# A two-layer Flamingo kernel: four more key and value units among the BitNet tiles, and three pairs of PSUM banks for the tiles instead of four

## What is computed

```python
x = x + tanh(g_xattn[0]) * L0_xattn(layernorm(x), ids, ctx, ctx, ctx)   # experts whose weights are the context
x = x + tanh(g_ffn[0])   * L0_ffn(layernorm(x), w_gate, w_up, w_down)   # BitNet: ternary weights, Hadamard
x = x + tanh(g_xattn[1]) * L1_xattn(layernorm(x), ctx, Wq, Wk, Wv, Wo)  # 16 heads of 128, 8 batches of 128
x = x + tanh(g_ffn[1])   * L1_ffn(layernorm(x), gate_w, ...)            # 32 routed experts, top 8, and a shared one

# L0_ffn:  inter = silu(bitlinear(x, w_gate)) * bitlinear(x, w_up);  out = bitlinear(hadamard(inter), w_down)
# L1_xattn: q = (x @ Wq) / sqrt(128);  k = ctx @ Wk;  v = ctx @ Wv
#           out = softmax(q k^T) v @ Wo
```

## Time and profile before

| | |
|---|---|
| median of three runs | 580.26 us |
| profiled execution | 581.05 us |
| its span on the core | 579.3 us |
| mean granted TensorE clock | 0.994 of full speed |
| busy: PE | 542.2 us (94%) |
| busy: DVE, ACT, POOL | 390.9, 349.3, 313.9 us |

### The profile page before, as it was taken

How to read it: one execution, slowest core, us unless ns; L and a number is a source line. 1 busy time by engine, 2 the same in 40 slices (tenths; PEclk the granted TensorE clock), 3 DMA queues, 4 the chain that set the end, 5 groups by cost and what they waited for, 6 DMA issues and landing times.

```text
span 579.3 us, 9617 instructions
## 1 busy us (share of the span) xinstructions
PE 542.2 (94%) x3242; PEld 464.7 (80%) x3242; DVE 390.9 (67%) x822; ACT 349.3 (60%) x719; POOL 313.9 (54%) x312
## 2 busy tenths in 40 slices
PE   2899998998989999999999999999999989898997
PEld 2677766777778898999999999999899767677884
DVE  6868986689755676555565767636765756867574
ACT  3633244657587868656575745746765664677574
POOL 1688238798177888443245433325786654852121
PEclk9999999999999999999999999989999999999999
DMA  8711244310256766787977677824546643345552
GB/s 255 261 55 54 83 136 159 134 37 1 78 200 215 227 209 201 232 237 263 274 224 241 196 261 220 247 81 145 180 149 176 217 140 127 98 154 172 173 175 71
DMA packets 67232, 97.88 MB, mean 169 GB/s; under 512 B 6384, under 2 KB 38896, under 8 KB 67184
## 3 DMA queue, kind: packets, MB, share of 16 engines
q1 hardware_dynamic: 67184, 97.26, 52.4%
HBM read 68.28 MB, written 28.97 MB: 168 GB/s over the span
## 4 chain that ended last, share of the span: by engine, by line
PE 71%; DVE 12%; ACT 6%; POOL 4%; issue 3%; DMA 2%; SPq 0%; DVEq 0%; POOLq 0%
PE ps L1519 20%; PE ps L1520 20%; PE ps L1521 20%; PE ps L1620 4%; PE ps L1726 2%; PE ps L1710 2%; DMA xr<-in_x 1%; DVE e_r L1446 1%; PE ps L1733 1%; DVE a_sel L1163 1%; DVE qtok L1200 1%; ACT q2T L899 1%; PE ps L1739 1%; DMA cw_row<-cw_scratch 1%; DVE st L1060 1%
## 5 line engine op out<-in xcount | busy, mean ns | idle before, releaser
L642 POOL TENSOR_TENSOR probs<-probs,rsum 128x512 f32<-128x512 f32 x64 | 66.4, 1041 | 81.0 <-DVE rsum L1229 80.9
L1224 DVE TENSOR_REDUCE nmax<-ps 128x2 f32<-128x512 f32 x64 | 44.1, 689 | 41.2 <-PE ps L1521 41.0
L1446 DVE SCALAR_TENSOR_TENSOR e_r<-ps,cw_row 128x512 f32<-128x512 f32 x64 | 43.8, 687 | 31.3 <-PE ps L1521 30.3
L1022 ACT ACTIVATE e_hi<-e_r 128x512 fp32r<-128x512 f32 x64 | 40.3, 629 | 40.3 <-DVE e_r L1446 40.0
L936 ACT ACTIVATE probs<-ps,nmax 128x256 f32<-128x256 f32 x128 | 59.6, 479 | 0.2
L569 POOL TENSOR_TENSOR kv_w_lo<-blk_raw,kv_w_hi 128x1024 fp32r<-128x1024 f32 x17 | 41.2, 2422 | 26.0 <-ACT kv_w_hi L807 26.0
L761 POOL TENSOR_TENSOR e_lo<-e_sq,e_hi 128x512 fp32r<-128x512 f32 x19 | 24.5, 1291 | 50.3 <-ACT e_sq L1028 47.8
L1220 DVE TENSOR_TENSOR oT_lo<-ps,oT_hi 128x512 fp32r<-128x512 f32 x32 | 22.1, 692 | 42.3 <-ACT oT_hi L946 42.3
L1215 DVE TENSOR_TENSOR pT_lo<-ps,pT_hi 128x512 fp32r<-128x512 f32 x64 | 43.8, 685 | 9.4 <-ACT pT_hi L942 8.7
L942 ACT ACTIVATE pT_hi<-ps 128x512 fp32r<-128x512 f32 x64 | 38.3, 600 | 19.5 <-PE ps L1620 19.4
L946 ACT ACTIVATE oT_hi<-ps 128x512 fp32r<-128x512 f32 x32 | 19.1, 597 | 43.0 <-PE ps L1521 43.0
(11 more groups left out here) (296 smaller groups left out, 1855.4 us busy)
## 6 DMA issues: line engine op xcount, KB each, us to landing
cw_row<-cw_scratch SPq DMA_DIRECT2D x64, 256.0 KB, 3.3
v_hl<-v_scratch SPq DMA_DIRECT2D x24, 512.0 KB, 3.7
blk_raw<-in_w_blocks SPq DMA_DIRECT2D x23, 512.0 KB, 4.4
k_hl<-k_scratch SPq DMA_DIRECT2D x18, 512.0 KB, 3.9
k_scratch<-kv_out SPq DMA_DIRECT2D x32, 256.0 KB, 2.6
v_scratch<-kv_out SPq DMA_DIRECT2D x32, 256.0 KB, 3.1
v_scratch<-kv_hi SPq DMA_DIRECT2D x24, 256.0 KB, 2.4
blk_raw<-in_w_tail SPq DMA_DIRECT2D x10, 512.0 KB, 4.7
```

Of the source, the lines that this page charges most:

```text
L642: nc.gpsimd.tensor_tensor(probs[:, b, :, :], probs[:, b, :, :], rsum[:, b, :].unsqueeze(2).to_broadcast([P, 2, S]), ALU.mult).then_inc(pro ...
L1022: nc.scalar.activation(e_hi[i % 4][:, :], e_r[i % 2][:, :], ACT.Square).then_inc(e_hi_done, 1)
L1224: V.tensor_reduce(nmax[:, b, :], ps[:, S_BANK[b], :].rearrange("p (t k) -> p t k", t=2), AX.X, ALU.max, negate=True).then_inc(max_done, 1)
L1446: V.scalar_tensor_tensor(e_r[i % 2][:, :], ps[:, UP_BANK[i % 4], :], 0.0, cw_row[i % 4][:, :], ALU.max, ALU.mult).then_inc(root_done, 1)
```

## The change

The tiles keep to three pairs throughout, and banks 0 and 1 stay with the units. Four new places hold one unit each: f2, f3, f4 and f5. The unit at d5 goes, and one of the two at d6. `FRONT_UNITS` becomes 24, and the attention's slots hold units 24 to 63: every unit in them moves two slots, one step, earlier (m0 holds unit 24 where it held unit 22), and the slots m21 and e21 stay empty. Units 22 and 23 (keys of heads 10 and 11) become raw ones. `STEP_OF_BLOCK` and the order in which blocks are split are as they were.

```diff
-        FILLS = {"a11": 1, "y2": 1, "y6": 4, "u0": 2, "g1": 1, "u1": 3, "f0": 3, "g2": 1, "f1": 2, "d4": 0, "d5": 1, "c6": 1, "d6": 2}
+        FILLS = {"a11": 1, "y2": 1, "y6": 4, "u0": 2, "g1": 1, "u1": 3, "f0": 3, "g2": 1, "f1": 2, "f2": 1, "f3": 1, "f4": 1, "f5": 1,
+                 "c6": 1, "d6": 1}
...
         for u in FFN:
-            if u == ("W", "f1"):
-                free.insert(0, 0)
-            elif u == ("W", "d4"):
-                free.remove(0)
-            elif u[0] not in "DWP":
+            if u[0] not in "DWP":
                 pair_of[u] = free.pop(0)
...
             load_block(8)
-            store("d5")
+            for n in range(2, 6):
+                store("f" + str(n))
             store("c6")
...
+                if 3 <= i <= 6:
+                    take("f" + str(i - 1))
                 if i == 2:
                     take("f1")
...
-                elif i == NT:
-                    take("d5")
...
-                    elif key == "d5":
-                        wait_freed(last_user[0])
...
-                        if b == 0:
-                            pe.wait_ge(kv_taken, FILL_AT["f1"][-1] + 1)
-                        elif b == 4:
+                        if b == 4:
```

## The result

The changed kernel takes 592.84 us in the median (591.13 to 595.67, 4 runs) against 580.01 us of the kernel before beside it (579.41 to 581.16): slower, ratio 1.0219 [1.018, 1.0259]. Run twice more beside the kernel before, it took 593.66 us against 579.26 (1.0253 [1.0215, 1.0292]) and 595.10 us against 579.94 (1.0266 [1.0233, 1.0298]). The forecast was 595.8 us. Five executions lie far outside their group (3021.26 us of three pairs only, its profiled one; 1081.67 and 1884.02 of the kernel before; 897.85 of "H7 covered"; 607.39 of "26 units in front"): the ratios leave them out, the medians in the table count them. The profiled execution took 591.13 us (span 589.3, mean granted clock 0.991), 10.1 us over the one of before.

What follows compares the result with a forecast made beforehand. TensorE was taken to bound the kernel, full in the attention and nearly full in the tiles. Terms 1.1 + 4.0 - 0.8 + 2.5 + 8.1 - 2.8 + 3.4 = +15.5 on 580.26 gave 595.8 us, range 590.5 to 599.0.

Steps and rivals of the forecast that it cites:

- The pairs: Tiles: with three pairs H1 waits until ScalarE has copied Q1's transposes, +1.1 us, bounds 0 and +1.65.
- I take 0: Steady tiles: G's and U's waits come within 0.1 us of TensorE's arrival, so 0, with +0.4 us for the range.
- The units at f: Units at f2 to f5, between F and D: 0.99 us each, +4.0 us together, covering the copy D waited for.
- The tail: Last tiles: units taken from d5 and d6 and less slowing of `ln_i` by GpSimd, -0.8 us, bounds -1.3 and -0.3.
- The slots: Attention: blocks 8, 11 and 13 are split too late for m0, m2 and m4, +2.5 us and +8.1 us.
- The empty slots: Attention step 21: two units fewer at 1.39 us each, -2.8 us, upper end 0.
- The clock: TensorE's clock falls once at m2 and once at m4, 1.7 us each, +3.4 us, bounds 0 and 6.8.
- the clock stays up: Rival: the three waits at m0, m2 and m4 come but the clock does not fall, 592.4 us, chance 0.24.
- Not slower: Rival: blocks 8, 11 and 13 are ready at m0, m2 and m4, no waits or falls, 581.8 us, chance 0.04.
- the upper end of the units: Units at f2 to f5: nothing is covered at D, 4 x 1.47 = +5.9 us.
- The chances of slower: Whole kernel: slower by over 0.3% (about 1.7 us), chance 0.95.

Runs made afterwards that it cites:

- three pairs only: Kernel before with three pairs of banks for the tiles and all units where they were: 583.03 us, ratio 1.0070; again 583.07 us, ratio 1.0071.
- H7 covered: The kernel on time, with ScalarE's copy of block 6 moved behind `qT` and the unit at c6 moved to d5: 578.25 us, ratio 0.9985.
- 26 units in front: H7 covered, with 26 front units (one each at f2 to f5, d4, d5, c6, d6), K3 split among the tiles, other blocks reordered: 579.77 us, ratio 0.9983.
- the kernel with two of them: The kernel on time with units at f2 and f3 only, 22 units in front: 583.40 us, ratio 1.0058.
- the kernel on time: Changed kernel with blocks K3 and V3 ahead of Q2 and O2, and block 8's high half copied ahead of two query products: 580.76 us, ratio 1.0015.

## Why the prediction was right, and where it was wrong

**The pairs.** H1: +1.1 predicted, +1.2 measured, and the releaser was `qT`. The step that failed is "I take 0" for the steady tiles: three pairs alone lengthen iterations 3 to 6 by 0.9 us each, since G waits for `q`. I had compared G's wait with the time at which TensorE gets there with a unit in front of it, where both agree to 0.1 us, and concluded that the pairs cost nothing. That holds only as long as a unit stands there. H1's term has a cause too that the prediction doesn't name: before `qT` ScalarE copies block 6, which it has to wait for (0.71 us in this trace), so that +1.2 is the value of this execution; in the third trace H1 waited 0.8 us more.

**The units at f.** +4.0 predicted, +3.5 measured; the sum was right and the payer wrong. They were priced by F to D with and without a unit, a real lengthening. But without them the same time is lost at G. (What a unit at f would cost with four pairs was not run.) So "the pairs cost 0 and the units 4.0" should have been "the pairs cost 3.5 and the units then cost 0", and taking units out would win nothing, as the kernel with two of them showed.

**The tail.** -0.8 predicted, -1.2 measured. P0 did hang on `hT_lo`. `ln_i` took 0.17 us instead of the 1.20 of before, with GpSimd's `k_hl` over before it started:

```profile
146.49 0.17 DVE L1069 TENSOR_SCALAR ln_i<-ln_v 128x4 int32<-128x4 int32 x1
```

```profile
144.70 1.73 POOL L573 TENSOR_TENSOR k_hl<-k_hl 128x512 fp32r<-128x512 f32 x1
```

**The slots.** Predicted 2.5 + 8.1; measured 2.6 + 4.1 + 4.0 without the falls. The distances between slot and split, read from before, carried over to 0.1 us. Two kernels took the waits away by moving the splits, and with the order of blocks their loads. The empty slots gave 2.65 of 2.8 us.

**The clock.** +3.4 predicted for two falls. In the first trace there were three, worth 1.5 + 1.4 + 1.3 = 4.2 us, and the two of the trace of before did not come again, -3.1. Net +1.1: together with -1.1 in the front and -1.3 at 522 us this is why the two profiled executions are only 10.1 us apart. The first group's median, +12.8, is of four executions and no trace takes it apart; the other two groups gave +14.4 and +15.2. The three traces of the changed kernel have three, four and seven falls. The rival "the clock stays up" (592.4 us) is the nearest to the first median and wrong in its mechanism, since the clock fell at all three waits, and at two of them in the second trace. That the forecast, +15.5, came within 2.7, 1.1 and 0.3 us of the three differences is in part luck: it leaves out how many falls an execution has at places that the change doesn't touch, while the executions of before alone lie between 575.71 and 582.83 us. The Trainium skill, TensorE: Matmul & The Clock Gate, section "Why this matters for your kernels", warns of idle gaps between bursts; the 3.71 us here agree with it (a fall in six of six). The falls after 1.86 to 2.56 us show that gaps shorter than it warns of can do it, and the measurement decides.

**Not slower.** That no unit waits for its block was given 0.04, and the kernel on time is what it describes: 580.8 us, where 581.8 was worked out.

**Small slips.** The prediction read the fall at 381 us as some 2.5 us behind the start of the small matmuls at 378.88; it began at 381.7, 2.8 us behind. The eight transposes, put at 0.80 us for the upper end of the units, take 0.87 in the rows (C at 115.75, F at 116.62), so that end is +5.6, not +5.9. The chances of slower add up to 0.94, not 0.95. None of them moves the forecast.

What stays open is why the same idle time was followed by a fall in one execution and not in another (below).

## What to carry to other kernels

When buffers are taken from a loop, price the loop with the buffers gone and nothing put in their place: an added piece of work and a buffer wait can lie on top of each other, and then the row that shows the one hides the other. When work is pulled forward in a fixed order, list what each piece needs and where that is made; here three splits that stayed put cost some 12 of the 13 to 15 us. Price idle time on TensorE together with the fall of the clock that may follow it, and read how many falls the trace of before has, since they need not come again.

## What the hardware showed

**Each fall had the same size.** Each fall inside the runs had the clock at half for 3.4 us, so that 1.7 us of full speed were not granted; twice two came in a row (6.8 us at half). It cost 1.3 to 1.6 us of time. The run time goes with the mean granted clock, in steps of about one fall: of the executions of before in the three groups, 23 at 0.990 or 0.991 took 581.2 us in the mean, 39 at 0.993 or 0.994 579.5, 10 at 0.996 or 0.997 578.0 and 2 at 0.999 575.8. Much of the spread of this kernel is the number of falls.

**When it fell.** Over the twelve traces of kernels with three pairs, by idle time ahead: at H1 none after 1.25 us (four traces) or 1.68 to 1.77 (four), a fall after 1.86, 1.96, 2.05 and 2.56; at H7 a fall after 1.52, 1.56 and 1.60 but none after 1.48, 1.53, 1.54, 1.54, 1.55 and 1.59; at m0 four of five after 2.45 to 2.47; at m2 and m4 six of six after 3.7. Two other places say the same: before the transposes of `h` near 466 us it fell after 2.04 and 2.12 and not in the eleven traces with 1.82 to 1.85; and before those near 22 us after 2.19 and not after 1.74 or less. Taken together, idle times of 1.86 to 2.6 us went with a fall in eleven of twelve cases. But in the kernel with 26 units in front 1.82 us ahead of scores(0, 0) did so too, and in three traces of thirteen it fell at F0, behind two idle times of some 1.2 us that stand 2.3 us apart. And it falls without idle time: the products with `gw` come in two runs of 24 matmuls of 32 columns, each run 2.6 us long, and behind the first (near 381 us) it fell in five traces of thirteen, behind the second (near 477 us) in nine.

**Four elements took 1.20 us.** `ln_i`, 128x4, needs 0.17 us by itself and 1.20 us when GpSimd's subtraction of 512 columns ran beside it and ended with it. That is one instance in one trace; the other twelve have 0.17 us. A second of the kind is in the kernel with 26 units in front: there the subtraction came later, `ln_i` took 0.17 and the instruction ahead of it, `ln_v` (128x4), 0.92 us instead of 0.53, and ended within 0.1 us of GpSimd's.
